# Sliding-window attention block on one core: score maxima as 64x64 matmul tiles with the band added by matmuls, and q and k stacked by 48-partition loads

## The reference, cut to what matters

```python
# B=8 sequences, S=1024, D=256, H=16 heads of 16, window W=64, FFN=1024, E=8 experts
xn = layernorm(x)
q, k, v = (xn @ Wq + bq), (xn @ Wk + bk), (xn @ Wv + bv)      # in blocks of 64 rows, 16 heads
kc, vc = [previous block, own block, next block]               # 192 keys for 64 queries
scores = q . kc / 4;  scores = where(|i + 64 - j| <= 64 and the key exists, scores, -1e9)
a = softmax(scores) @ vc @ Wo + bo
h = layernorm(a + xn) * g1 + b1
f = gelu(h @ W1 + c1) @ W2 + c2
attn_out = layernorm(f + h) * g2 + b2
chosen = argmax(xn @ gate_w.T)                                 # one of 8 experts per row
return x + attn_out + xn + expert_w[chosen] @ xn
```

## Time and profile before

| what | value |
|---|---|
| median of the three timed executions | 1550.31 us (1548.87 to 1557.77) |
| the profiled execution, first to last instruction | 1553.1 us |
| PE busy | 1240.9 us (80%), 10696 matmuls |
| VectorE busy | 1071.5 us (69%) |
| ScalarE busy | 739.8 us (48%) |
| GpSimd busy | 739.9 us (48%) |
| mean DMA rate | 87 GB/s |

### The profile page before, as it was taken

The page is one execution under the profiler, slowest core; times in us unless marked ns, Lnnn a source line. Parts: engine busy times, 40 slices in busy tenths (PEclk is TensorE's granted clock), DMA queues, the critical chain, the costliest instruction groups (busy, mean ns, idle before and its releaser), DMA issues.

```text
span 1553.1 us, 34323 instructions
## 1 busy us (share of the span) xinstructions
PE 1240.9 (80%) x10696; PEld 714.8 (46%) x10696; DVE 1071.5 (69%) x3743; ACT 739.8 (48%) x1356; POOL 739.9 (48%) x749
## 2 busy tenths in 40 slices
PE   0648885999678985999859997689858898599967
PEld 0424452735346353654527454373535535265435
DVE  8656775777757775867757677576766676587565
ACT  1305744366543744447443565426544374445642
POOL 6443745156531766037550474406752177504661
PEclk9959997999989997989979899798988899799979
DMA  7463056220733119130462206422082212912010
GB/s 237 92 139 118 3 117 122 76 92 29 144 79 100 57 69 166 50 112 13 108 131 69 99 8 145 91 83 83 33 156 75 88 57 74 162 48 94 2 28 28
DMA packets 89647, 135.00 MB, mean 87 GB/s; under 512 B 10209, under 2 KB 62305, under 8 KB 87393
## 3 DMA queue, kind: packets, MB, share of 16 engines
q1 hardware_dynamic: 83328, 115.91, 30.0%
q0 software_dynamic: 6144, 16.79, 4.4%
HBM read 74.47 MB, written 59.90 MB: 87 GB/s over the span
## 4 chain that ended last, share of the span: by engine, by line
PE 49%; DMA 17%; issue 11%; POOL 8%; DVE 8%; SPq 3%; ACT 3%; DVEq 0%; POOLq 0%; ACTq 0%
DMA pair_dram<-pool 9%; PE bank L1132 8%; PE bank L1035 8%; PE bank L1154 8%; PE bank L1036 7%; PE bank L1038 7%; PE bank L1181 6%; DMA q_s<-q_s 5%; DVE xn L604 2%; SPq L284 2%; DMA ys_dram<-xn 2%; PE bank L1102 2%; POOL x_sb L453 2%; POOL x_sb L451 2%; POOL rs L386 2%
## 5 line engine op out<-in xcount | busy, mean ns | idle before, releaser
L713 DVE CUSTOM_DVE_ANT_0 bank<-bank,mask 128x192 f32<-128x192 f32 x1024 | 337.3, 388 | 199.1 <-PE bank L1132 195.1
L943 ACT ACTIVATE pool<-bank 128x512 f32<-128x512 f32 x512 | 293.0, 597 | 118.9 <-PE bank L1154 113.2
L1132 PE MATMUL bank<-k_s,q_s 128*64 128x192 f16 x2048 | 175.3, 269 | 144.1 <-DMA q_s<-q_s 141.2
L440 POOL TENSOR_SCALAR_AFFINE_SELECT pool<-pool 128x512 f32<-128x512 f32 x256 | 172.2, 675 | 194.1 <-ACT pool L943 193.4
L1154 PE MATMUL bank<-q_s,k_s 128*128 128x256 f16 x1024 | 199.3, 290 | 28.7 <-issue 21.3
L389 POOL TENSOR_TENSOR rs<-ve,neghalf 128x1 f32<-128x1 f32 x64 | 36.9, 577 | 384.8 <-DVE ve L776 384.8
L1132 PEld LDWEIGHTS bank<-k_s,q_s 128*64 128x64 f16 x2048 | 77.8, 113 | 250.1 <-issue 226.9
L1181 PE MATMUL bank<-pool,v_a 128*32 128x256 f32 (+2 forms) x2560 | 161.1, 345 | 19.9 <-DVE pool L727 8.6
L989 ACT ACTIVATE pool<-bank,c1c 128x512 f32<-128x512 f32 x128 | 87.8, 686 | 169.5 <-PE bank L1038 132.5
L790 DVE TENSOR_TENSOR pool<-pool 128x512 f16<-128x512 f32 x128 | 106.7, 839 | 63.3 <-ACT pool L955 62.2
L713 DVE DVE_READ_ACCUMULATOR2_ANT m_sb<- 128x1 f32 x1024 | 144.6, 141 | 0.3
(11 more groups left out here) (149 smaller groups left out, 2511.1 us busy)
## 6 DMA issues: line engine op xcount, KB each, us to landing
pair_dram<-pool SPq DMA_DIRECT2D x32, 512.0 KB, 7.6
xn<-xs_dram SPq DMA_DIRECT2D x40, 384.0 KB, 3.7
ys_dram<-xn SPq DMA_DIRECT2D x120, 128.0 KB, 1.7
q_s<-pair_dram SPq DMA_DIRECT2D x48, 256.0 KB
k_s<-pair_dram SPq DMA_DIRECT2D x48, 256.0 KB
x_sb<-in_L_attn_x SPq DMA_DIRECT2D x8, 1024.0 KB, 5.7
res_dram<-x_sb SPq DMA_DIRECT2D x8, 1024.0 KB, 4.8
res_r<-res_dram SPq DMA_DIRECT2D x8, 1024.0 KB, 7.4
```

Source lines behind the costliest of these rows:

```text
L440: nc.gpsimd.affine_select(out=p, in_=p, compare_op=ALU.is_ge, fill=0.0, base=0, pattern=[[0, 4], [1, 2 * W]], channel_multiplier=-1).then_ ...
L713: ins = nc.vector.tensor_tensor_reduce(out=SB[u % 2][:, i * WIN:i * WIN + WIN], in0=SB[u % 2][:, i * WIN:i * WIN + WIN], in1=mask[:, v, :] ...
L943: nc.scalar.activation(prob[:, (k + 2) % 3, 2 * pu:2 * pu + 2, :], TB[u % 2][:, :].rearrange("p (h q) -> p h q", h=2), ACT.Exp, scale=EXP_ ...
L1132: mm = nc.tensor.matmul(SB[u % 2][W * bl:W * bl + W, i * WIN:i * WIN + WIN], q_s[:, h, W + w0:2 * W + w0], k_s[:, h // 2, w0:w0 + WIN], st ...
```

## The change

`q_s` and `k_s` both hold two heads in a column range, even heads on partitions 0 to 63 and odd ones on 64 to 127. Each of the stacks is stored to `pair_dram` with its three slots laid out as 48 rows (the high part is stored twice), and loaded with 48 partitions in one transfer: 12 stores and 8 loads in a turn in place of 4 stores, 12 loads and 2 copies. The columns of Wq and Wk are permuted on the host for this. q and k of heads 0 to 7 are made first (units 0 to 3), and step 0 of `scores` waits only for their four loads; step 16 waits for the other four. ScalarE's wait before it writes over `qk_h` is for both halves.

`scores` reads 48 partitions (the row of the maxima is left out, so nothing is set back to zero) and writes 64 PSUM partitions per matmul. The band is added by `mask_mm`, a matmul with an identity of 64 and a mask of 256 columns, accumulated onto the two outer thirds of the scores: four more matmuls in a step. VectorE's maximum is one plain reduction over two heads. `scores_t` reads the 64 partitions of its head. In steps 1 to 18 each `scores_t` matmul of one half of the partitions is followed by two `scores` matmuls of the other half. GpSimd's preparation clears a `q_s` of half the size and builds smaller masks and the identity.

```diff
-    pair_dram = nc.dram_tensor("pair_dram", (2, 4, P, S), F16, kind="Internal").ap()
+    pair_dram = nc.dram_tensor("pair_dram", (2, 2, 4, 2, 3, HD, S), F16, kind="Internal").ap()
...
-        mask = sb("mask", [P, 3, WIN], BF16)
+        ident16 = sb("ident16", [P, W], BF16)
+        mask = sb("mask", [P, 3, 2, W], BF16)
...
-        q_s = sb("q_s", [P, H, S + 2 * W], F16)
+        q_s = sb("q_s", [P, H // 2, S + 2 * W], F16)
...
-        NSTACK = 2 * 2 * 3 + 2
-        stack = count("stack", 16 * NSTACK)
-        pair_st = count("pair_st", 16 * 4)
+
+        stack = [count(f"stack{i}", 16 * 4) for i in range(2)]
+        pair_st = [count(f"pair_st{i}", 16 * 6) for i in range(2)]
...
+            def pair_stores(b, i):
+
+                c, qk = divmod(i, 2)
+                for src, done, slots in ((qk_h, qk_hi, (0, 2 if qk else 1)), (qk_l, qk_lo, (1 if qk else 2,))):
+                    sp.wait_ge(done.sem, done.at(b, 2 * i + 2))
+                    for slot in slots:
+                        sp.dma_start(pair_dram[c, qk, :, :, slot, :, :].rearrange("j a d s -> d (j a) s"),
+                                     src[:, 2 * qk + c, :]).then_inc(pair_st[i % 2].sem, 16)
+
+            def stack_loads(b, i):
+
+                c, qk = divmod(i, 2)
+                sp.wait_ge(pair_st[i % 2].sem, pair_st[i % 2].at(b, 48 * (i // 2 + 1)))
+                dst = k_s if qk else q_s
+                for a in range(2):
+                    sp.dma_start(dst[W * a:W * a + KW, 4 * c:4 * c + 4, W:W + S],
+                                 pair_dram[c, qk, :, a, :, :, :].rearrange("j o d s -> (o d) j s")).then_inc(stack[c].sem, 16)
+
             def stacks(b):
 
-                for qk in range(2):
-                    for half, (src, done) in enumerate(((qk_h, qk_hi), (qk_l, qk_lo))):
-                        sp.wait_ge(done.sem, done.at(b, 4 * qk + 4))
-                        sp.dma_start(pair_dram[half, 2 * qk:2 * qk + 2].rearrange("o p s -> p o s"),
-                                     src[:, 2 * qk:2 * qk + 2, :]).then_inc(pair_st.sem, 16)
-                    sp.wait_ge(pair_st.sem, pair_st.at(b, 32 * (qk + 1)))
-
-                    for a in range(2):
-                        for slot in range(3):
-                            low = slot == (1 if qk else 2)
-                            src = pair_dram[int(low), 2 * qk:2 * qk + 2].rearrange("c (j a d) s -> a d (c j) s", a=2, d=HD)[a]
-                            r = W * a + HD * slot
-                            dst = k_s[r:r + HD, :, W:W + S] if qk else q_s[r:r + HD, a:H:2, W:W + S]
-                            sp.dma_start(dst, src).then_inc(stack.sem, 16)
-
-                for a in range(2):
-                    r = W * a + 3 * HD
-                    sp.dma_start(q_s[r:r + 1, a:H:2, W:W + S], q_s[r:r + 1, 1 - a:H:2, W:W + S]).then_inc(stack.sem, 16)
+                pair_stores(b, 0)
+                for i in range(1, 4):
+                    pair_stores(b, i)
+                    stack_loads(b, i - 1)
+                stack_loads(b, 3)
...
-                    sp.dma_start(q_s[r:r + 1, 4 * g + a:4 * g + 4:2, W:W + S],
+                    sp.dma_start(q_s[r:r + 1, 2 * g:2 * g + 2, W:W + S],
...
+            step(nc.gpsimd.memset(ident16[:, :], 0.0))
             for a in range(2):
-                part = mask[W * a:W * a + W, :, :]
+                rows_a = slice(W * a, W * a + W)
+                step(nc.gpsimd.affine_select(out=ident16[rows_a, :], in_=ident16[rows_a, :], compare_op=ALU.not_equal, fill=1.0,
+                                             base=0, pattern=[[-1, W]], channel_multiplier=1))
+                part = mask[rows_a, :, 0, :]
                 step(nc.gpsimd.affine_select(out=part, in_=part, compare_op=ALU.is_ge, fill=NEG, base=0,
-                                             pattern=[[0, 3], [1, WIN]], channel_multiplier=-1))
-                step(nc.gpsimd.affine_select(out=part, in_=part, compare_op=ALU.is_ge, fill=NEG, base=2 * W,
-                                             pattern=[[0, 3], [-1, WIN]], channel_multiplier=1))
+                                             pattern=[[0, 3], [1, W]], channel_multiplier=-1))
+                part = mask[rows_a, :, 1, :]
+                step(nc.gpsimd.affine_select(out=part, in_=part, compare_op=ALU.is_ge, fill=NEG, base=0,
+                                             pattern=[[0, 3], [-1, W]], channel_multiplier=1))
...
-                    o, hf = divmod(u, 2)
+                    o, hf = u % 4 // 2 * 2 + u // 4, u % 2
...
             def maxima(b, j):
 
                 g, t = divmod(j, T)
-                v = 0 if t == 0 else 2 if t == T - 1 else 1
-                for pu in range(2):
-                    u = 2 * j + pu
-                    dve.wait_ge(S_ps.sem, S_ps.at(b, u + 1))
+                for n, par in enumerate((1, 0)):
+                    dve.wait_ge(S_ps.sem, S_ps.at(b, 2 * j + n + 1))
                     dve.sem_inc(passed, 1)
-                    for i in range(2):
-                        h = 4 * g + 2 * pu + i
-                        ins = nc.vector.tensor_tensor_reduce(
-                            out=SB[u % 2][:, i * WIN:i * WIN + WIN], in0=SB[u % 2][:, i * WIN:i * WIN + WIN], in1=mask[:, v, :], scale=1.0,
-                            scalar=-3.0e38, op0=ALU.add, op1=ALU.max, accum_out=m_sb[:, h, t:t + 1])
-                    ins.then_inc(mx.sem, 1)
+                    nc.vector.tensor_reduce(m_sb[:, 4 * g + par:4 * g + 4:2, t],
+                                            SB[par][:, 0:2 * WIN].rearrange("p (h c) -> p h c", h=2), AX.X, ALU.max).then_inc(mx.sem, 1)
...
-                for pu in range(2):
-                    u = 2 * k + pu
-                    act.wait_ge(ST_ps.sem, ST_ps.at(b, u + 1))
-                    nc.scalar.activation(prob[:, (k + 2) % 3, 2 * pu:2 * pu + 2, :], TB[u % 2][:, :].rearrange("p (h q) -> p h q", h=2),
+                for par in range(2):
+                    act.wait_ge(ST_ps.sem, ST_ps.at(b, 2 * k + par + 1))
+                    nc.scalar.activation(prob[:, (k + 2) % 3, par::2, :], TB[par][:, :].rearrange("p (h q) -> p h q", h=2),
...
-                    act.wait_ge(pair_st.sem, pair_st.at(b + 1, 64))
+                    for stored in pair_st:
+                        act.wait_ge(stored.sem, stored.at(b + 1, 96))
+                        act.sem_inc(passed, 1)
...
-            def scores(b, j, first=False, half=None):
+            def edge(n):
+
+                return 0 if n == 0 else 2 if n == 2 * T - 1 else 1
+
+            def score_mm(out, n, j, par, i):
 
                 g, t = divmod(j, T)
-                if j == 0 and not half:
+                h, r = 2 * g + i, slice(W * par, W * par + KW)
+                q = W + (2 * t + n) * W
+                return nc.tensor.matmul(out[W * n:W * n + W, i * WIN:i * WIN + WIN], q_s[r, h, q:q + W], k_s[r, h, q - W:q + 2 * W],
+                                        start=i == 0, stop=False, skip_group_check=True)
+
+            def score_t_mm(out, k, par, i):
+
+                g, t = divmod(k, T)
+                h, r = 2 * g + i, slice(W * par, W * par + W)
+                return nc.tensor.matmul(out[:, i * QW:i * QW + QW], k_s[r, h, W + t * P:W + t * P + P], q_s[r, h, t * P:t * P + QW],
+                                        start=True, stop=True)
+
+            def mask_mm(out, n, t, par):
+
+                r = slice(W * par, W * par + W)
+                band = mask[r, edge(2 * t + n), :, :].unsqueeze(1).broadcast_to([W, 2, 2, W])
+                dst = out[W * n:W * n + W, 0:2 * WIN].rearrange("p (h c k) -> p h c k", h=2, c=3)[:, :, 0::2, :]
+                return nc.tensor.matmul(dst, ident16[r, :], band, start=False, stop=True, skip_group_check=True)
+
+            def scores_wait(b, j, par, first=False):
+
+                u = 2 * j + (1 if par == 0 else 0)
+                if j == 0 and par == 1:
                     pe.wait_ge(route.sem, route.at(b, 6))
-                    pe.wait_ge(stack.sem, stack.at(b, 16 * NSTACK))
-                for pu in range(2) if half is None else (half,):
-                    u = 2 * j + pu
-                    if not first or u >= 2:
-                        pe.wait_ge(mx.sem, mx.at(b, u - 1))
-                    for i in range(2):
-                        h = 4 * g + 2 * pu + i
-                        for bl in range(2):
-                            w0 = (2 * t + bl) * W
-                            mm = nc.tensor.matmul(SB[u % 2][W * bl:W * bl + W, i * WIN:i * WIN + WIN],
-                                                  q_s[:, h, W + w0:2 * W + w0], k_s[:, h // 2, w0:w0 + WIN],
-                                                  start=True, stop=True)
-                    mm.then_inc(S_ps.sem, 1)
+                    pe.sem_inc(passed, 1)
+                    pe.wait_ge(stack[0].sem, stack[0].at(b, 64))
+                    pe.sem_inc(passed, 1)
+                if j == 2 * T and par == 1:
```

(57 more changed lines are left out.)

14 lines of the change are left out of this document (7 added, 7 removed).

## The result

The changed kernel takes 1814.6 us (median of four, 1813.4 to 1818.3), the kernel before beside it 1552.6: a ratio of 1.170, interval 1.166 to 1.173. The prediction was 1400 with a range of 1375 to 1572. It missed by 415 us, and no rival comes near: the highest figure named, R1 with the stack term at its low end, is 1590. Medians and ratios here leave out executions that are over 1.5% longer than the fastest of the same kernel; there are two such, both in experiment 13.

What follows compares the result with a forecast made beforehand. PE, busy 80% of the span, was taken as the bound, with its stack wait and the attention loop. Savings of 84 (stacks), 5 (outer scores), 58 (loop) and 4 (preparation), 151 us, gave 1400 us, range 1375 to 1572.

Steps and rivals of the forecast that it cites:

- R1: Loop steps 1 to 18: form changes paid inside each bank, 0.975 against 0.61 us, 105 us lost, 1562 in all; chance 0.31.
- the stack term at its low end: Stack transfers: the lower bound of the gain per turn, 8 us instead of 11.9; with R1 it gives 1590.
- The loop, -58 us forecast: Steps 1 to 18: halves run together with free form changes, 0.40 us saved a step, 58 us, bounds -105 and 79.
- the rival with the price inside the bank: The same as R1: four form changes of 0.12 us in each bank of steps 1 to 18; chance 0.31.
- The stacks, -84 us forecast: Step 0's wait for stack transfers, 16.9 us a turn, goes; 11.9 net of give-backs, 84 us in seven turns.
- GpSimd's two long operations: W1 stage: L466 and L468, 4.51 us each, hold VectorE; 2 us lost each, 4 a turn, bounds 0 and 6.
- The other hold, 3.4 forecast: W1 stage: GpSimd's L495 holds VectorE's L688, so PE waits for unit 5 from near 969.1 to 972.5, 3.4 us.
- the 2.4 us for a warm clock: After the stack wait: PE no longer starts cold, so the first two units give 2.4 us back a turn.
- The steps of scores outside the loop, -5 us: 14 steps a turn: four array quarters side by side take 0.40 us in place of 0.45, 5 us saved.
- Two reductions a step: VectorE in the loop: the profile after would show two maxima reductions a step near 0.55 us.
- The preparation, -4 us: First turn's preparation: clearing half the array saves 3.9 us on the path.
- 0.15 for slower: Whole kernel: chance of a slower result, taken from the part of R1 above 1566 us.

Runs made afterwards that it cites:

- experiment 13: Changed kernel with all scores of a step together, GpSimd's long sums in tiles and 12 unread matmuls ahead of loop step 1: 1493.8 us, ratio 0.965.
- experiment 9: Changed kernel with a burst of 24 unread matmuls of 512 columns ahead of loop step 3: 1846.8 us, one run.
- experiment 1: Kernel before with only its loop interleaved head by head as in the change, 128 rows, one semaphore instruction a bank added: 1794.2 us, ratio 1.154.
- experiment 10: experiment 1 with a burst of 24 unread matmuls of 512 columns ahead of loop step 3: 1667.7 us, one run.
- experiment 3: Kernel before with the new stack transfers, unit order and half-head waits alone; scores, maxima and masks untouched: 1528.0 us, ratio 0.982.
- experiment 5: experiment 3 with GpSimd's three long sums and one product cut into eight pieces each: 1447.4 us, ratio 0.935.
- experiment 6: experiment 3 with both kinds of score matmul reading 64 rows, banks by head parity, four semaphore instructions a step added: 1706.7 us, ratio 1.103.
- experiment 7: experiment 3 with only the transposed scores reading 64 rows, banks by head parity, four semaphore instructions a step added: 1704.7 us, ratio 1.100.
- experiment 4: Changed kernel with all eight scores and four masks of a loop step issued together between two pairs of transposed scores: 1682.3 us, ratio 1.082.

## Why the prediction was wrong

**The loop, -58 us forecast, 284 lost.** This step failed, in two pieces.

*Forms.* I assumed that going from the 64x128 form to the 64x64 form costs nothing. The warm steps of experiment 9 show the rival with the price inside the bank to be right nearly to the digit: 0.93 us a bank against its 0.975, 2.44 a step against 2.52. A transposed score (0.11 by its columns) takes 0.21 here, a pair of scores (0.08) 0.20. By that mechanism the loop loses 18 x (2.44 - 1.79) x 8 = 94 us. (The price from which R1 decides comes out at 0.110 us a change, not 0.108; that changes nothing.) I had put 0.31 on it and held against it that "every change seen keeps 128 rows"; that had no bearing, since experiment 1's order with 128 rows pays the same 0.10 us a change when warm (experiment 10). The Trainium skill, TensorEngine Tiling (Array Packing), section Key Properties, was the better guide here. By it a change of tiling mode drains the engine, and the 0.10 us that each change costs in these rows agrees. The rule on weight loads of another row group, from the same skill's TensorE: Matmul & The Clock Gate, Part 3, does not show in these rows: in experiment 9 the matmuls of the other form start 0.20 to 0.21 us behind a transposed one, though they read the other rows, the same as at 128 rows in experiment 10.

*Clock.* This was in no case at all. I took durations from rows at 1.00 and used them for the whole loop. The rest of the 284, 190 us, is the loop running at 0.50: at half clock the step is 3.93, at full clock 2.44. In the kernel before, the stretches already showed the loop entered at 0.50, with three steps of 2.0 to 2.9 us and then the rise. I read the cold clock at W1 and not here, where an edit that changes what PE does right after a pause can decide whether the clock ever rises. What raises and keeps it, as the runs show:

| loop's matmuls | comes in at 0.50 | comes in at 1.00 (turns 0 and 7) | after a burst, at 1.00 | us a step cold, warm |
|---|---|---|---|---|
| before: 128 rows, grouped | rises in step 3 | stays | - | 2.8, 1.79 |
| 128 rows, interleaved | stays | falls by step 2 | keeps | 3.51, 2.25 |
| 64 rows, transposed scores alone | stays | falls by step 2 | not run | 3.00 |
| 64 rows, quarters together | stays | falls by step 2 | keeps from step 3 on | 2.77, 1.79 |
| the change: 64 rows, interleaved | stays | falls by step 2 | falls | 3.93, 2.44 |

In experiments 3 and 5, whose loop is that of before, the clock of turn 0 falls too in step 2, but is back in step 3; the others do not come back. Experiments 1, 6 and 7 show that interleaving and fewer rows, each with its added semaphore instructions, suffice to prevent the rise. What the chip goes by was not measured and stays open. The share of busy time on the page does not tell: it is 5.00 of 5.00 us in the changed loop and 26.00 of 26.00 in that of before.

Warm, the quarters together take 1.79 us a step, exactly what before takes. So even the best order of the changed matmuls saves PE nothing in the loop: of that step 0.10 to 0.22 us is a wait for the maxima's bank, and masks and changes of form use up what the rows gave.

**The stacks, -84 us forecast, 35 gained in that stage.** The wait did go; that the loads land in time was right, and so was, in kind but not in size, that holds of VectorE by GpSimd come back in its place. I took 4 us a turn for GpSimd's two long operations, by PE's slack of one or two units, with 6 as the bound. In the changed kernel PE waits 7.7 us there. What I left out is the order on VectorE: both its sums are held, the maxima queue behind them, and the score bank that PE needs next is freed by the maxima. The other hold, 3.4 forecast, came as 4.7 in the turn shown, but on the routing (L667), not on the operation named (L688). And behind a pause of 7.68 us the clock was at 0.50 again (938.9 to 945.8), so most of the 2.4 us for a warm clock did not come. 11.9 - 3.7 - 1.3 - 2.4 = 4.5 us a turn, against 3.2 in the turn shown and 5.1 in the mean of seven. Experiment 5 shows the mechanism: nothing changes but the size of GpSimd's pieces, and 81 us come back, though not all in this stage.

**The steps of scores outside the loop, -5 us.** Right. The chain that ended last, in the changed kernel:

```profile
924.74 0.29 PE bank L1134 x8
925.03 0.11 PE bank L1149 x4
925.14 0.32 PE bank L1042
```

Eight scores and four masks in 0.40 us, as worked out: quarters of one form do run at once.

**VectorE.** Two reductions a step at 556 ns (forecast 0.55). Right; as PE was the bound in the loop, it gained nothing there.

**The preparation, -4 us.** PE's wait for GpSimd's first fills is 21.0 us where it was 25.0. Right.

**The chances.** 0.15 for slower came from one mechanism's high end; nothing in the range allowed for a clock that doesn't rise.

## What to carry to other kernels

Before changing the shape or order of matmuls, mark where the engine comes in cold and where the clock rises; price the new mix at half clock as well, and put "it never rises" among the cases. Put matmuls of different forms in groups, and count each change of form at about 0.1 us at full clock even when the forms read different rows. Cut long GpSimd operations that run beside VectorE's into pieces, and when a wait is taken away, look at what is queued on the engine that will be waited for next.

## What the runs showed of the hardware

- Four matmuls of 256 columns a step that read 64 rows in place of 128 keep the granted clock at 0.50 through 18 steps, at the same busy time (1704.7 against 1528.0 us; the slower kernel also has four short semaphore instructions a step more).
- The clock has a memory: one and the same mix stays at 0.50 when it starts there (2.77 us a step) and at 1.00 when a burst has raised it (1.79). Work that nobody reads, some 7 us a turn, made the kernel 104 us faster (one run). In steps 1 to 3 the same mix can lose a raised clock (experiments 4 and 13).
- VectorE was held for as long as a GpSimd instruction ran, up to 4.8 us at a time, and got in between two pieces of under 1 us. GpSimd's own work took 12.9 in place of 9.4 us for it.
- A change between forms of matmul costs 0.10 us at the clock of 1.00, at 128 rows (experiment 10) and between 64x128 and 48x64 on other rows (experiment 9).
- Whether the mixes that were run without a burst (64 rows in groups, 64 rows in the order of before) would keep a raised clock beyond step 3 stays open; so does what the added semaphore instructions do to it by themselves.
